# Expert layers: second-layer weights read by TensorE at a register's address in place of VectorE's copy

## The chip, the core and the metric

The kernel runs on one core of a Trainium2 chip. A core has five engines that run their own instruction streams and meet through semaphores: TensorE (PE; its weight loads are listed as PEld), VectorE (DVE), ScalarE (ACT), GpSimd (POOL) and SyncE (SP), which here issues transfers. Each engine has a sequencer in front of it that waits, branches, computes registers and issues; the profile writes a q behind the engine's name for it (DVEq, SPq, PEldq). The metric is the device time of one execution in microseconds (us).

## The reference, cut to what matters

The network has 14 blocks, four of them mixtures of experts: every token is sent to its best expert (first layer, `L0_ffn`, used twice) or to its best two (second layer, `L1_ffn`, used twice).

```
def _moe_mlp(x, gate_w, gate_b, w1, w2):                    # L0: 4096 tokens of 128, 8 experts, hidden 512
    one_hot = one_hot(argmax(xf @ gate_w + gate_b), E)
    h = gelu(einsum('td,edh->teh', xf, w1), approximate=True)
    y = einsum('teh,ehd->ted', h, w2)
    out = einsum('te,ted->td', one_hot, y)
...
def _moe(x, gate_w, gate_b, W1, b1, W2, b2):                # L1: the best two, weighted
    top_v, top_i = top_k(softmax(xt @ gate_w + gate_b), 2)
    for e in range(E):
        h = gelu(xt @ W1[e] + b1[e], approximate=False) @ W2[e] + b2[e]
        out = out + combine[:, e:e + 1] * h
```

The kernel holds x as 16 sequences of 256 tokens, 32 tiles of 128 tokens.

## The kernel before, in words

`experts` (L1237) is called four times: `e00_` and `e01_` with `top=1`, `e10_` and `e11_` with `top=2`. First it routes: each token's row goes by an indirect transfer to a place in the table `routed` in HBM, so that the rows of one expert lie together. Then comes the loop that this case is about, over NT tiles of 128 routed rows: NT is `TILES * top + 7`, 39 in e00 and e01, 71 in e10 and e11, 220 in all. The loops are written out in full. Which expert a tile belongs to is known only on the chip: `tables` writes it into `expert_i`, and the tile's place in `routed` into `offset_i`.

For tile j, named by what the trace writes:

- SP (L1353, L1354): waits until tile j-4 has been given out (`got` is a ring of four), loads the tile's place from `offset_i` into a register (a `value_load`: TENSOR_LOAD, FUSED_REGOPS, SEQ_ASSERT), and issues the transfer `e_got<-routed`.
- PE, one pass: `turn(j)` (L1734, e_F) waits for the transfer and transposes the rows; `hidden_layer(j-1)` (L1741, e_H) multiplies the tile before by `W1s`; `output(j-2)` (L1750, e_Y) multiplies the one before that by `W2s`. A float32 product of one block stands in the trace as two weight loads and two matmuls, so e_H and e_Y have eight each.
- ACT: copies e_F into `xT` (L1440, L1443) and applies the activation (L1449 in e00 and e01; L1453, four pieces with a bias, in e10 and e11).
- DVE, one pass: `weights(j)` loads the expert's number from `expert_i` into a register (L1601), copies the bias `b1s` (L1605, e10 and e11 alone), copies the expert's first layer from `core.W1` into `W1s` (L1608) and its second layer from `core.W2` into `W2s` (L1611), one of three buffers. Then `give(j-2)` makes the row addresses of the result (L1618, L1620, e_back), adds the second bias (L1624, e_biased, e10 and e11 alone) and writes `e_y` (L1628).
- POOL: sends `e_y` to the table `results` by an indirect transfer (L1397). After tiles 1, 5, 9 and so on to 29 it also adds a group of `core.Y` to `core.X` (L1401), and in e10 and e11 a bias row (L1406).

The stationary operand of e_Y is `hidden`; the weights of the second layer are the moving one. PE reads `W1s` and `W2s` at addresses that stand in the program. `core.W1` and `core.W2` hold all eight experts of a layer in SBUF.

Of the kernel before, what the change touches and what calls it, by code (L numbers as in the profile page):

```python
# [15 lines left out]
P = 128  # L16
SEQS, L, D = 16, 256, 128
# [44 lines left out]
def allocator(nc, ctx, prefix):  # L62

    held = []

    def clear():
        nc.clear_and_free_semaphores(held)
        nc.all_engine_barrier()

    ctx.callback(clear)  # L70

    def sb(name, shape, dt=F32):
        return ctx.enter_context(nc.sbuf_tensor(prefix + name, shape, dt))

    def ps(name, shape=(P, 512), dt=F32):
        return ctx.enter_context(nc.psum_tensor(prefix + name, list(shape), dt))

    def sig(name, per=1, lead=0):
        sem = nc.alloc_semaphore(prefix + name)
        held.append(sem)  # L80
        return Signal(sem, per, lead)

    return sb, ps, sig
# [49 lines left out]
def await_(eng, signal, count):  # L133
    if count > 0:
        eng.wait_ge(signal.sem, count)
# [1101 lines left out]
def experts(nc, core, name, *, affine, normed_in, w_loaded, gate, gate_b, act_fn, top, b1=None, b2=None,  # L1237
# [7 lines left out]
    E, FC = 8, 4  # L1245
# [4 lines left out]
    with ExitStack() as ctx:  # L1250
        sb, ps, sig = allocator(nc, ctx, name)
# [3 lines left out]
        YB = [ps("Y0"), ps("Y1")]  # L1255
# [28 lines left out]
        expert_i = sb("expert_i", [P, NT], I32)  # L1284
# [4 lines left out]
        got = sb("got", [P, RING, W])  # L1289
        xT = sb("xT", [P, 2, P])  # L1290
        W1s = sb("W1s", [P, 2, FC * P])
        W2s = sb("W2s", [P, 3, FC, D])
        b1s = sb("b1s", [P, 3, FC]) if b1 is not None else None
        b2_all = sb("b2_all", [P, E, D]) if b2 is not None else None
        biased = sb("biased", [P, 2, D]) if b2 is not None else None
# [1 line left out]
        hidden = sb("hidden", [P, 2, FC, P])  # L1297
# [15 lines left out]
        counted, count_made, offsets_made, tables_made = (sig("counted"), sig("count_made"), sig("offsets_made"),  # L1313
                                                          sig("tables_made"))
        fetched = [sig(f"fetched{b}") for b in range(RING)]
        x_made, x_taken = sig("x_made"), sig("x_taken")
        w1_copied, w2_copied, hid_made, acted, y_made, y_taken, back_ready = (
            sig("w1_copied"), sig("w2_copied"), sig("hid_made"), sig("acted"), sig("y_made"), sig("y_taken"),
            sig("back_ready"))
        given = sig("given")  # L1320
        y_sent = [sig(f"y_sent{b}") for b in range(RING)]
# [142 lines left out]
        def _(dve):  # L1464
            steps = 0

            def step(ins):
                nonlocal steps
                ins.then_inc(dve_step.sem, 1)
                steps += 1  # L1470

            def settle():
                dve.wait_ge(dve_step.sem, steps)
# [124 lines left out]
            expert = {}  # L1598

            def weights(j):  # L1600
                e = expert[j] = dve.value_load(expert_i[0:1, j:j + 1], min_val=0, max_val=E - 1)  # L1601
                await_(dve, hid_made, j - 1)
                if b1 is not None:
                    await_(dve, acted, j - 2)
                    step(dve.tensor_copy(b1s[:, j % 3], core.b1[:].rearrange("p (e f) -> p e f", e=E)  # L1605
                                         [:, bass.ds(e, 1), :].rearrange("p o f -> p (o f)")))
                    settle()
                dve.tensor_copy(W1s[:, j % 2], core.W1[:, bass.ds(e, 1), :].rearrange("p o f -> p (o f)"))\  # L1608
                    .then_inc(w1_copied.sem, 1)
                await_(dve, y_made, j - 2)  # L1610
                dve.tensor_copy(W2s[:, j % 3], core.W2[:, bass.ds(e, 1)].rearrange("p o c d -> p (o c) d"))\  # L1611
                    .then_inc(w2_copied.sem, 1)

            def give(j):

# [33 lines left out]
            for j in range(NT + 2):  # L1649
                if j < NT:  # L1650
                    weights(j)
                if j >= 2:
                    give(j - 2)
# [40 lines left out]
        @block.tensor  # L1694
        def _(pe):
            def rank_tokens(g):

                pe.wait_ge(chosen.sem, g + 1)
                pe.wait_ge(based.sem, g + 1)
                await_(pe, placed, g)  # L1700
                pe.matmul(RB[:, 0:GT * E], core.ones16[:], before16[:, g % 2, None, :].to_broadcast([P, GT, E]),
                          start=True, stop=False)
                for back_by in range(1, GT):
                    pe.matmul(RB[:, back_by * E:GT * E], core.ones16[:], taken_by[:, g % 2, 0:GT - back_by, :],
                              start=False, stop=False)
                pe.matmul(RB[:, 0:GT * E], core.earlier16[:], taken_by[:, g % 2], start=False, stop=True)\
                    .then_inc(ranked.sem, 1)

            for g in range(GROUPS + 1):
                if g >= 1:  # L1710
                    rank_tokens(g - 1)
                if g < GROUPS:
                    if normed_in:
                        pe.wait_ge(normed.sem, normed.at(g, GT))
                    await_(pe, h_taken, g - 1)
                    for t in range(GT):
                        src = rows[:, 0, g % 2, t, 0:D] if normed_in else core.Y[:, g * GT + t, :]
                        ins = pe.transpose(F[g % 2][:, t * P:(t + 1) * P], src, core.ident[:])
                    ins.then_inc(h_made.sem, 1)
                    pe.wait_ge(h_taken.sem, g + 1)  # L1720
                    await_(pe, logit_taken, g)
                    for t in range(GT):
                        ins = pe.matmul(LB[:, t * E:(t + 1) * E], hT[:, g % 2, t * P:(t + 1) * P], gate[:],
                                        start=True, stop=True)
                    ins.then_inc(logit_made.sem, 1)
            pe.wait_ge(placed.sem, GROUPS)
            pe.wait_ge(based.sem, GROUPS + 1)
            pe.matmul(RB[:, 0:E], core.ones16[:], before16[:, GROUPS % 2, :], start=True, stop=True)\
                .then_inc(count_made.sem, 1)

            def turn(j):
                pe.wait_ge(fetched[j % RING].sem, 16 * (j // RING + 1))
                await_(pe, x_taken, j - 1)
                pe.transpose(F[j % 2][:, 0:P], got[:, j % RING, 0:D], core.ident[:]).then_inc(x_made.sem, 1)  # L1734

            def hidden_layer(j):
                pe.wait_ge(x_taken.sem, j + 1)
                pe.wait_ge(w1_copied.sem, j + 1)
                await_(pe, acted, j - 1)
                for f in range(FC):  # L1740
                    ins = pe.matmul(H[j % 2][:, f * P:(f + 1) * P], W1s[:, j % 2, f * P:(f + 1) * P], xT[:, j % 2],  # L1741
                                    start=True, stop=True)
                ins.then_inc(hid_made.sem, 1)

            def output(j):
                pe.wait_ge(acted.sem, j + 1)
                await_(pe, y_taken, j - 1)
                pe.wait_ge(w2_copied.sem, j + 1)
                for f in range(FC):
                    ins = pe.matmul(YB[j % 2][:, 0:D], hidden[:, j % 2, f], W2s[:, j % 3, f, :],  # L1750
                                    start=f == 0, stop=f == FC - 1)
                ins.then_inc(y_made.sem, 1)

            for j in range(NT + 2):
                if j < NT:
                    turn(j)
                if 1 <= j <= NT:
                    hidden_layer(j - 1)
                if j >= 2:
                    output(j - 2)  # L1760
# [737 lines left out]
def network(nc, a, out):  # L2498
    core = Core()
    with ExitStack() as ctx:  # L2500
# [36 lines left out]
        def l0_experts(n, prefetch=None):  # L2537
            experts(nc, core, f"e0{n}_", affine=(col("L0_ffn_ln2_w"), col("L0_ffn_ln2_b")), normed_in=True,
                    w_loaded=(core.moe_loaded.sem, 32), gate=core.gates[:, 0, :], gate_b=core.gate_b[:, 0, :],
                    act_fn=ACT.Gelu_apprx_tanh, top=1, prefetch=prefetch)  # L2540

        def l1_experts(n):
            experts(nc, core, f"e1{n}_", affine=None, normed_in=False, w_loaded=(core.moe_loaded.sem, 64),
                    gate=core.gates[:, 1, :], gate_b=core.gate_b[:, 1, :], act_fn=ACT.Gelu, top=2,
                    b1=core.b1, b2=a["b2"], out_norm=(row("L1_ffn_ln2_g"), row("L1_ffn_ln2_b")))
# [147 lines left out]
```

## Time and profile before

| | us |
|---|---|
| median of 3 runs | 5303.79 |
| lowest and highest | 5299.88, 5307.32 |
| the profiled execution | 5306.9 |
| its span, first to last instruction | 5305.2 |

| engine | busy us | share of the span | instructions |
|---|---|---|---|
| PE | 3913.4 | 74% | 25840 |
| PEld | 2745.5 | 52% | 25840 |
| DVE | 3560.2 | 67% | 9744 |
| ACT | 2366.2 | 45% | 5537 |
| POOL | 2394.7 | 45% | 3900 |

No engine is busy all the time, and the 14 blocks follow one another with a barrier between them, so a change inside `experts` is read from the four stretches in which its loop runs. They lie at about 972 to 1078, 2192 to 2303, 3181 to 3407 and 5017 to 5247 us, some 674 us of the span. Busy time leaves out sequencer work (register operations, waits, issues); only the rows that are asked for by a source line show those.

### The profile page before, as it was taken

To read this page: it belongs to the slowest core of one execution; us is meant where nothing else is said; L and a number is where in the kernel's file an instruction comes from. 1 tells how busy PE (TensorE), PEld (TensorE's weight loads), DVE (VectorE), ACT (ScalarE), POOL (GpSimd) and SP (SyncE) were. 2 spreads that over 40 slices of the span, in tenths; PEclk is the share of its full clock that TensorE was granted. 3 is DMA by queue.
4 is the path that set the end of the run, shared out by engine and by line. 5 is a ranking of instruction groups with operands and counts; after the bars stand their busy time and mean duration, and the time that the engine had idled before them with its cause. 6 is when DMAs were issued, how large, how long until landed. Compare 5 with 4: busy or idle time off the path is not lost. (4 is left out here: it accounts for less than half of the span.)

```text
span 5305.2 us, 89506 instructions
## 1 busy us (share of the span) xinstructions
PE 3913.4 (74%) x25840; PEld 2745.5 (52%) x25840; DVE 3560.2 (67%) x9744; ACT 2366.2 (45%) x5537; POOL 2394.7 (45%) x3900
## 2 busy tenths in 40 slices
PE   5889786679999787558868826457786887787364
PEld 3666464556666465446646526422333664455263
DVE  5787675656666675656657757669997664676566
ACT  2444464255555465234435514345552553355142
POOL 3656442433343442446633244367775661232542
PEclk9999898889999899789979959879998999899597
DMA  5000232100000232133313211212222330232112
GB/s 218 0 0 0 95 115 80 43 24 1 1 0 1 81 115 77 38 114 108 104 70 108 90 38 40 64 48 62 64 64 69 111 106 1 87 107 72 41 40 74
DMA packets 243672, 341.35 MB, mean 64 GB/s; under 512 B 26848, under 2 KB 185968, under 8 KB 242224
## 3 DMA queue, kind: packets, MB, share of 16 engines
q1 hardware_dynamic: 230064, 309.19, 17.5%
q0 software_dynamic: 13184, 27.22, 1.5%
q8 instruction: 179, 2.93, 0.2%
q14 instruction: 245, 2.01, 0.1%
HBM read 182.77 MB, written 147.26 MB: 62 GB/s over the span
## 5 line engine op out<-in xcount | busy, mean ns | idle before, releaser
L507 DVE TENSOR_REDUCE l0att_rowmax<-l0att_S 128x2 f32<-128x512 f32 x512 | 339.7, 686 | 144.7 <-PE l0att_S L678 143.7
L507 DVE TENSOR_REDUCE l1ffn_rowmax<-l1ffn_S 128x2 f32<-128x512 f32 x512 | 340.9, 686 | 134.5 <-PE l1ffn_S L678 133.1
L869 POOL TENSOR_TENSOR wb_prob<-wb_prob,wb_rden 128x128 f32<-128x128 f32 (+1 forms) x512 | 248.9, 508 | 378.3 <-DVE wb_rden L1046 378.0
L1397 POOL DMA_INDIRECT results<-e_y,e_back x220 | 216.1, 982 | 417.0 <-DVE e_y L1628 398.2
L1943 POOL TENSOR_TENSOR ssm_hc<-core_AW_all,ssm_Cs 128x512 f32<-128x512 f32 x256 | 321.2, 1271 | 129.6 <-DVE core_AW_all L2089 96.5
L911 ACT ACTIVATE wb_prob<-wb_biased,wb_nmax 128x128 f32<-128x128 f32 (+1 forms) x512 | 228.6, 447 | 254.2 <-DVE wb_nmax L1039 251.3
L2188 PE MATMUL ssm_Y<-ssm_hc,core_ident 128*128 128x512 f32 x512 | 290.8, 679 | 56.0 <-POOL ssm_hc L1943 29.8
L678 PE MATMUL l1ffn_S<-l1ffn_K,l1ffn_Q 128*128 128x512 f32 x512 | 253.5, 499 | 96.2 <-DVE l1ffn_rowmax L507 58.7
L2089 DVE TENSOR_TENSOR_SCAN core_AW_all<-core_AW_all,ssm_U 128x512 f32<-128x512 f32 x256 | 310.2, 1212 | 1.4 <-ACT core_AW_all L2032 1.4
L678 PE MATMUL l0att_S<-l0att_K,l0att_Q 128*128 128x512 f32 x512 | 249.3, 490 | 59.7 <-DMA l0att_K<-bounce 52.1
L2032 ACT ACTIVATE core_AW_all<-ssm_dt,ssm_A 128x510 f32<-128x510 f32 x256 | 178.5, 716 | 221.6 <-DVE core_AW_all L2089 220.0
L1039 DVE CUSTOM_DVE_ANT_0 wb_biased<-wb_S,wb_added 128x128 f32<-128x128 f32 (+1 forms) x512 | 162.6, 355 | 168.1 <-PE wb_S L1142 124.2
L1382 POOL DMA_INDIRECT routed<-e_rows,e_pos_i x192 | 188.3, 981 | 155.2 <-DVE e_pos_i L1556 104.1
L1734 PE MATMUL e_F<-core_ident,e_got 128*128 128x128 f32 x220 | 73.2, 333 | 244.7 <-DMA e_got<-routed 232.5
L484 ACT ACTIVATE core_AW_all<-l1ffn_T 128x512 f32<-128x512 f32 x256 | 151.8, 597 | 211.0 <-PE l1ffn_T L691 209.1
L1741 PE MATMUL e_H<-e_xT,e_W1s 128*128 128x128 f32 x1760 | 245.9, 285 | 0.0
L1750 PE MATMUL e_Y<-e_W2s,e_hidden 128*128 128x128 f32 x1760 | 238.3, 280 | 0.7 <-ACT e_hidden L1453 0.7
L911 ACT ACTIVATE wa_prob<-wa_biased,wa_nmax 128x128 f32<-128x128 f32 (+1 forms) x256 | 114.3, 447 | 250.6 <-DVE wa_nmax L1039 250.5
L1741 PEld LDWEIGHTS e_H<-e_xT,e_W1s 128*128 128x128 f32 x1760 | 224.7, 200 | 0.4
L484 ACT ACTIVATE core_AW_all<-l0att_T 128x512 f32<-128x512 f32 x256 | 149.1, 597 | 163.9 <-PE l0att_T L691 162.1
L1750 PEld LDWEIGHTS e_Y<-e_W2s,e_hidden 128*128 128x128 f32 x1760 | 220.2, 197 | 1.2 <-ACT e_hidden L1453 1.1
L2082 DVE TENSOR_TENSOR ssm_U<-ssm_du,ssm_B 128x512 f32<-128x512 f32 x256 | 177.8, 695 | 57.3 <-POOL ssm_du L1934 38.0
(499 smaller groups left out, 11841.5 us busy)
## 6 DMA issues: line engine op xcount, KB each, us to landing
bounce<-l0att_parts SPq DMA_DIRECT2D x128, 256.0 KB, 2.8
bounce<-l1ffn_parts SPq DMA_DIRECT2D x128, 256.0 KB, 2.8
ssm_Cs<-c_rows SPq DMA_DIRECT2D x128, 256.0 KB
routed<-core_Y SPq DMA_DIRECT2D x8, 2048.0 KB, 23.5
l0att_Q<-bounce SPq DMA_DIRECT2D x128, 128.0 KB
l0att_K<-bounce SPq DMA_DIRECT2D x128, 128.0 KB
bounce<-l1att_parts SPq DMA_DIRECT2D x64, 256.0 KB, 2.8
l1ffn_Q<-bounce SPq DMA_DIRECT2D x128, 128.0 KB
```

The costliest lines, as they stand in the source:

```text
L484: act.activation(probT[jp][:, kt, m, :, q0:L], T[u % 4][:].rearrange("p (j q) -> p j q", j=2)[:, :, q0:L], ACT.Exp)\
L507: dve.tensor_reduce(out=rowmax[:, jp, qt, 2 * pair:2 * pair + 2], in_=S[a % 2][:].rearrange("p (j k) -> p j k", j=2)[:, :, 0:keys(qt)], op ...
L678: ins = pe.matmul(out[:, :, 0:keys(qt)], Q[:, n % 2, jp, pair, tile(qt)], K[:, n % 2, jp, :, pair, 0:keys(qt)], start=not causal, stop=Tru ...
L869: ins = pool.tensor_tensor(out=prob[:, w_ % 4, a:b], in0=prob[:, w_ % 4, a:b], in1=rden[:, w_ % 4, n:n + 1].to_broadcast([P, b - a]), op=A ...
L911: ins = act.activation(prob[:, w_ % 4, a:b], biased[:, w_ % 2, a:b], ACT.Exp, scale=-1.0, bias=nmax[:, w_ % 4, n:n + 1], accum_out=total[: ...
L1382: pool.indirect_dma_start(core.routed, bass.IndirectOffsetOnAxis(ap=pos_i[:, g % 2, k, t:t + 1], axis=0), rows[:, k, g % 2, t, :], None).t ...
L1397: pool.indirect_dma_start(core.results, bass.IndirectOffsetOnAxis(ap=back[:, j % RING, 1:2], axis=0), y[:, j % RING, :], None).then_inc(y_ ...
L1741: ins = pe.matmul(H[j % 2][:, f * P:(f + 1) * P], W1s[:, j % 2, f * P:(f + 1) * P], xT[:, j % 2], start=True, stop=True)
L1750: ins = pe.matmul(YB[j % 2][:, 0:D], hidden[:, j % 2, f], W2s[:, j % 3, f, :], start=f == 0, stop=f == FC - 1)
L1943: pool.tensor_tensor(out=hc[:, u % 4], in0=hs[:, u % 4], in1=Cs[:, n % 4], op=ALU.mult)\
L2089: dve.tensor_tensor_scan(hs[:, u % 4], dA[:, u % 4], BU[u % 2][:], 0.0, ALU.mult, ALU.add)\
L2188: pe.matmul(YS[c][:], core.ident[:], hc[:, u % 4], start=n == 0, stop=n == N - 1)\
```

## The change

The copy of the second layer's weights, its three buffers and its semaphore are taken out of VectorE's `weights(j)`. TensorE's matmuls of `output` take their moving operand from `core.W2` itself, at an address worked out from a register that holds the tile's expert. TensorE fills that register with a `value_load` of its own, for tile j right behind `turn(j)`, and waits once ahead of its loop for `offsets_made`.

```diff
-        W2s = sb("W2s", [P, 3, FC, D])
...
                 dve.tensor_copy(W1s[:, j % 2], core.W1[:, bass.ds(e, 1), :].rearrange("p o f -> p (o f)"))\
                     .then_inc(w1_copied.sem, 1)
-                await_(dve, y_made, j - 2)
-                dve.tensor_copy(W2s[:, j % 3], core.W2[:, bass.ds(e, 1)].rearrange("p o c d -> p (o c) d"))\
-                    .then_inc(w2_copied.sem, 1)
...
+            expert = {}
+
             def output(j):
+
+                e = expert.pop(j)
                 pe.wait_ge(acted.sem, j + 1)
                 await_(pe, y_taken, j - 1)
-                pe.wait_ge(w2_copied.sem, j + 1)
                 for f in range(FC):
-                    ins = pe.matmul(YB[j % 2][:, 0:D], hidden[:, j % 2, f], W2s[:, j % 3, f, :],
+                    ins = pe.matmul(YB[j % 2][:, 0:D], hidden[:, j % 2, f],
+                                    core.W2[:, bass.ds(e, 1), f, :].rearrange("p o d -> p (o d)"),
                                     start=f == 0, stop=f == FC - 1)
                 ins.then_inc(y_made.sem, 1)
 
+            pe.wait_ge(offsets_made.sem, 1)
             for j in range(NT + 2):
                 if j < NT:
                     turn(j)
+                    expert[j] = pe.value_load(expert_i[0:1, j:j + 1], min_val=0, max_val=E - 1)
                 if 1 <= j <= NT:
                     hidden_layer(j - 1)
                 if j >= 2:
```

On PE, in the steady part of the loop of e00, one pass stood like this before (F is the transpose, H the first layer, Y the second; ISA is a register operation):

```order
L1734 MATMUL e00_F0<-core_ident,e00_got 128x128
L1741 MATMUL e00_H1<-e00_xT,e00_W1s 128x128 x4
L1750 MATMUL e00_Y0<-e00_W2s,e00_hidden 128x128 x4
L1734 MATMUL e00_F1<-core_ident,e00_got 128x128
L1741 MATMUL e00_H0<-e00_xT,e00_W1s 128x128 x4
```

and stands like this with the change:

```order
L1730 MATMUL e00_F0<-core_ident,e00_got 128x128
L1758 TENSOR_LOAD e00_expert_i
L1758 ISA x2
L1737 MATMUL e00_H1<-e00_xT,e00_W1s 128x128 x4
L1749 ISA
L1749 MATMUL e00_Y0<-core_W2,e00_hidden 128x128
L1749 ISA
L1749 MATMUL e00_Y0<-core_W2,e00_hidden 128x128
L1749 ISA
L1749 MATMUL e00_Y0<-core_W2,e00_hidden 128x128
L1749 ISA
L1749 MATMUL e00_Y0<-core_W2,e00_hidden 128x128
```

Three instructions now stand between the transpose and the first layer, and one register operation ahead of each matmul of the second layer.

On DVE, one pass of e10 stood like this before:

```order
L1601 TENSOR_LOAD e10_expert_i
L1601 ISA x2
L1605 ISA
L1605 COPY e10_b1s<-core_b1 128x4
L1608 ISA
L1608 COPY e10_W1s<-core_W1 128x512
L1611 REGISTER_ALU
L1611 COPY e10_W2s<-core_W2 128x512
L1618 TENSOR_TENSOR e10_back<-e10_got,e10_keep_i 128x1
```

and with the change:

```order
L1600 TENSOR_LOAD e10_expert_i
L1600 ISA x2
L1604 ISA
L1604 COPY e10_b1s<-core_b1 128x4
L1607 ISA
L1607 COPY e10_W1s<-core_W1 128x512
L1614 TENSOR_TENSOR e10_back<-e10_got,e10_keep_i 128x1
```

The copy and its register operation are gone; VectorE still loads the expert's number itself. ACT, POOL and SP keep their instructions.

## Rows read from the trace of the kernel before

**Rows 1.** The loop of e00: who waited for whom, total us, times, longest.

```profile
PE e_F L1734 <- DMA e_got<-routed: 29.1, 23, 9.3
DVE e_y L1628 <- PE e_Y L1750: 22.1, 20, 1.8
```

**Rows 2.** In time order, e00: start us, us, engine line op, [idle before <-releaser].

```profile
1016.44 1.06 PE L1750 MATMUL e_Y<-e_W2s,e_hidden 128*128 128x128 f32 x8
1017.53 0.35 DVE L1628 TENSOR_SCALAR e_y<-e_Y,e_got 128x128 f32<-128x128 f32 x1 [0.42 <-PE e_Y L1750]
1018.28 0.43 DVE L1608 COPY e_W1s<-core_W 128x512 f32 x1 [0.40 <-issue]
1018.80 0.33 PE L1734 MATMUL e_F<-core_ident,e_got 128*128 128x128 f32 x1 [1.30 <-DVE e_W1s L1608]
1018.96 1.07 PE L1741 MATMUL e_H<-e_xT,e_W1s 128*128 128x128 f32 x8
1019.86 1.06 PE L1750 MATMUL e_Y<-e_W2s,e_hidden 128*128 128x128 f32 x8
1020.76 0.27 PE L1734 MATMUL e_F<-core_ident,e_got 128*128 128x128 f32 x1
...
1024.02 0.33 PE L1734 MATMUL e_F<-core_ident,e_got 128*128 128x128 f32 x1 [1.20 <-DMA e_got<-routed]
```

**Rows 3.** SP's value_load by its line, one tile: ns min/median/max, start us.

```profile
L1353 SPq TENSOR_LOAD <-e_offset_i x1: 268/268/268, 1005.3 to 1005.3; - x1
L1353 SPq FUSED_REGOPS  x1: 152/152/152, 1005.6 to 1005.6; - x1
L1353 SPq SEQ_ASSERT  x1: 18/18/18, 1005.8 to 1005.8; - x1
L1354 SPq FUSED_REGOPS  x1: 42/42/42, 1005.9 to 1005.9; - x1
```

**Rows 4.** VectorE's value_load by its line, one tile, and the e_y ahead of it.

```profile
1006.73 0.35 DVE L1628 TENSOR_SCALAR e_y<-e_Y,e_got 128x128 f32<-128x128 f32 x1 [0.16 <-issue]
L1601 DVEq TENSOR_LOAD <-e_expert_i x1: 302/302/302, 1006.7 to 1006.7; - x1
L1601 DVEq FUSED_REGOPS  x1: 190/190/190, 1007.1 to 1007.1; - x1
L1608 DVEq FUSED_REGOPS  x1: 57/57/57, 1007.4 to 1007.4; - x1
```

**Rows 5.** PE's sequencer by line: waits of e00's loop, register operations of another block.

```profile
L135 PEldq EVENT_SEMAPHORE  x1: 51/51/51, 1018.8 to 1018.8; - x1
L1748 PEldq EVENT_SEMAPHORE  x1: 51/51/51, 1018.9 to 1018.9; - x1
L821 PEldq FUSED_REGOPS  x12: 50/50/50, 119.7 to 1591.4; - x12
L821 DVEq FUSED_REGOPS  x12: 62/63/69, 120.3 to 1595.8; - x12
```

**Rows 6.** DVE in time order, loop of e10, two passes of a group of four.

```profile
3255.85 0.61 DVE L1608 COPY e_W1s<-core_W 128x512 f32 x1
3256.39 0.41 DVE L1611 COPY e_W2s<-core_W 128x512 f32 x1
3256.71 0.15 DVE L1618 TENSOR_TENSOR e_back<-e_got,e_keep_i 128x1 uint32<-128x1 uint32 x1
...
3261.16 0.17 DVE L1605 COPY e_b1s<-core_b 128x4 f32 x1 [0.55 <-issue]
3261.47 1.98 DVE L1608 COPY e_W1s<-core_W 128x512 f32 x1
3263.38 1.50 DVE L1611 COPY e_W2s<-core_W 128x512 f32 x1
3264.80 0.14 DVE L1618 TENSOR_TENSOR e_back<-e_got,e_keep_i 128x1 uint32<-128x1 uint32 x1
```

**Rows 7.** PE in time order: the ends of that group, and two tiles further on.

```profile
3254.99 0.33 PE L1734 MATMUL e_F<-core_ident,e_got 128*128 128x128 f32 x1 [2.76 <-DMA e_got<-routed]
...
3268.51 0.33 PE L1734 MATMUL e_F<-core_ident,e_got 128*128 128x128 f32 x1 [2.93 <-DMA e_got<-routed]
...
3295.65 0.33 PE L1734 MATMUL e_F<-core_ident,e_got 128*128 128x128 f32 x1 [2.89 <-DMA e_got<-routed]
...
3301.28 0.33 PE L1734 MATMUL e_F<-core_ident,e_got 128*128 128x128 f32 x1 [0.59 <-DMA e_got<-routed]
```

**Rows 8.** POOL in time order, in the same group.

```profile
3261.88 1.28 POOL L1401 TENSOR_TENSOR core_X<-core_X,core_Y 128x512 f32<-128x512 f32 x1
3263.24 1.35 POOL L1406 TENSOR_TENSOR core_X<-core_X,core_rows 128x512 f32<-128x512 f32 x1
```

More of the change, by code:

```diff
@@ L1316, in experts @@
         x_made, x_taken = sig("x_made"), sig("x_taken")
-        w1_copied, w2_copied, hid_made, acted, y_made, y_taken, back_ready = (
-            sig("w1_copied"), sig("w2_copied"), sig("hid_made"), sig("acted"), sig("y_made"), sig("y_taken"),
+        w1_copied, hid_made, acted, y_made, y_taken, back_ready = (
+            sig("w1_copied"), sig("hid_made"), sig("acted"), sig("y_made"), sig("y_taken"),
             sig("back_ready"))
```

## The prediction

> **What bounds the kernel now.** The change touches only the expert loops, so I read the list of waits inside one loop first, then the time order of each engine there. The waits of e00 [rows 1] show that PE is not short of work but of data: before 23 of its 39 transposes (e_F) it sits idle until the fetched rows land, 29.1 us in all, while DVE waits for PE's e_Y in 20 passes. Neither is the bound by itself. They form a ring with SP's transfer, because `got` has four buffers and the fetch of tile j+4 waits until tile j has been given out. Follow it in [rows 2]. PE's pass with e_F at 1018.80 ends its e_Y at 1020.92 (1019.86 + 1.06), so the PE part is 2.12 us. From the end of an e_Y to the e_F that it lets go: e_Y of 1016.44 ends at 1017.50, e_y is written from 1017.53 to 1017.88, and the transpose of that chain starts at 1020.76 at the latest, with the one at 1024.02 following from the e_Y that ended at 1020.92. That is 3.10 to 3.26 us. The ring spans two tiles (tile j is given out in the pass of tile j+2 and releases tile j+4), so a tile costs (2.12 + 3.15) / 2 = 2.64 us, near what the passes at 1018.80, 1020.76 and 1024.02 show: 5.22 us for two. PE alone could do a pass in 1.96 us.
>
> In e10 and e11 DVE has more to do. In the first 32 tiles the groups of four take 13.52 us (3254.99 to 3268.51) [rows 7]. In one pass of each group DVE's two copies stretch from 0.61 and 0.41 us to 1.98 and 1.50 us [rows 6], and both end 0.3 us after one of POOL's additions does [rows 8]. Behind them everything on DVE is late, e_y with it, and PE waits 2.93 us. Past tile 32 POOL adds nothing, and the ring rules: 3295.65 to 3301.28 is 5.63 us for two tiles, 2.82 each.
>
> **The change, part by part.**
>
> *Taken from DVE.* One copy a tile. Without a stall it holds up the next instruction for 0.32 us (3256.39 to 3256.71 [rows 6]), with one for 1.42 us (3263.38 to 3264.80). In e00 and e01 that buys nothing: DVE idles 0.42 us ahead of the e_y of 1017.53, waiting for PE [rows 2], and it is PE that it waits for in 20 passes [rows 1]. Past tile 32 in e10 and e11 the ring rules as well. In the 16 groups of the first 32 tiles (8 in each of e10, e11) DVE is the late one: its chain of 13.52 us loses 3 x 0.32 + 1.42 = 2.4 us and comes to 11.1 us a group. What is late next there is the ring, below. The first-layer copy keeps its stall of about 1.4 us.
>
> *The lock.* Both stretched copies end 0.3 us behind a POOL addition [rows 6, 8]. The Trainium skill ("SBUF — State Buffer", section "Who interferes with whom") says that a VectorE copy in a 2-port mode and a GpSimd instruction exclude each other for a whole instruction; by that rule, and the trace agrees, one of the two stalls in each group goes with the copy and the other stays.
>
> *Put on PE: the value_load.* Three sequencer instructions a tile, behind e_F and ahead of e_H. No row shows them on PE, so I bound them by the two engines that do them. On SP they take 268, 152 and 18 ns, 0.44 us bare; with the gaps between them, from the start of the load at 1005.3 to the next instruction at 1005.9, some 0.57 us [rows 3]. On DVE it is 0.64 us (1006.7 to 1007.4) [rows 4]. I take SP's 0.57, since for one and the same register operation PE needs 50 ns where DVE needs 63 [rows 5], so PE's sequencer is of the quicker kind. The ends are 0.44 and 0.64.
>
> *Is it hidden?* A pass hides it only if the sequencer can do it while PE still works or still waits. DVE's load starts at 1006.7, when the wait of the e_y ahead of it is over (1006.73) and not before [rows 4]. On PE the wait instruction that stands behind e_F runs at 1018.8, with the e_F of 1018.80 itself [rows 5, 2], though what it waits for besides had nearly all come earlier. So I take it that the sequencer stands at e_F until the rows have landed, and the load begins then. PE has emptied its queue by that time (it was idle 1.30 us), so e_H starts 0.57 us later than now. Even a pass such as that of 1020.76, with no idle time ahead, began about when its rows landed, since each fetch goes out right behind an e_y. I count the load in full in nearly every pass.
>
> *Put on PE: four register operations* ahead of the matmuls of e_Y, some 50 ns each [rows 5] with a gap like SP's 40 ns, 0.09 us apiece and 0.36 us in all. The sequencer now comes by ahead of e_Y (L1748) at 1018.9, while its first matmul starts at 1019.86 [rows 5, 2]: a lead of 0.9 us, because e_H runs for 0.9 us in between. The load moves both alike, so the lead stays and covers them. If the cover were gone they would cost 0.36 us a pass. The moving operand's size stays, so the eight matmuls keep their pace: nothing. The wait for `offsets_made` stands ahead of transposes that wait for transfers which wait for it as well: nothing.
>
> *The sum.* 0.57 us more in PE's part of a ring over two tiles is 0.285 us a tile.
> - e00 and e01: 78 tiles x 0.285 = +22 us.
> - e10 and e11 past tile 32: 78 x 0.285 = +22 us.
> - e10 and e11, first 32 tiles: the ring is now 2.82 + 0.285 = 3.10 us a tile, 12.4 us a group, and covers DVE's 11.1. Against 13.52 that is -1.1 x 16 groups = -18 us.
> - Sum +26 us. A few passes whose rows land early hide the load; I take 1 off: +25. On the profiled execution's 5306.9 that is 5332; the median is 3.1 lower, so 5329.
>
> With 0.44 us the terms are +17, +17 and -1.4 x 16 = -22: +12. With 0.64: +25, +25 and -1.0 x 16 = -16: +34. So 5316 to 5338 for this case.
>
> **The rivals.**
>
> *The load runs while e_F waits (faster).* If the sequencer only hands e_F to a queue and goes on, the load is over when the rows land, at least where PE was idle. For it: PE's sequencer does come by ahead of e_Y 0.9 us early. Against it: the two starts above. Then the e00, e01 and late terms are 0, and a group falls to the ring's 4 x 2.82 = 11.3 us or DVE's 11.1, less gain where the remaining stall shows: -1.7 to -2.2 x 16 = -28 to -36, so about 5273. The Trainium skill ("Perfetto Trace Analysis", section "Tensor Engine Instruction") describes just this: the sequencer pushes an instruction into a wait queue and is ready for the next before the semaphore is met. DVE's load in [rows 4] doesn't start as early as that would let it. 13%.
>
> *The address operations are not covered (slower still).* A matmul whose operand is at a register's address may be taken one at a time, each behind its register operation. Then 0.36 us a pass comes on top, 0.18 us a tile, x 220 = +40: 5370. It decides when one matmul with its operation takes the sequencer longer than the 0.22 us that PE needs for a block, and the lead of 0.9 us is used up. No row shows such a matmul. 14%.
>
> *The load costs less, or DVE's relief reaches further.* The loss in 156 tiles and the gain in 64 pull against each other; with 0.35 us of load exposed the terms are +14, +14 and -1.6 x 16 = -25, about +3: 5307. 13%.
>
> **How the numbers follow.** The forecast, 5316 to 5338, gets 60%; the three rivals 13, 14 and 13%. Predicted 5329, the likeliest case's time. The range of 5296 to 5372 takes in all but the hidden load (13%) and some 5% above. A change of 0.2%, 10.6 us, is about what a measurement of this kernel can tell from none. Slower by more: the forecast and the second rival, nearly whole, 73%. Within: the third, 13%. Faster: the first and a little of the third, 14%.
>
> **What would show it.** In the changed kernel PEldq would have TENSOR_LOAD, FUSED_REGOPS and SEQ_ASSERT of about 268, 152 and 18 ns, the first starting with e_F; from e_F to the first e_H 0.73 us, where it is 0.16 now [rows 2]; e_H to e_Y still 0.90 us; two tiles in the ring of e00 about 5.8 us in place of 5.2; the loops of e00 and e01 some 11 us longer each. The groups of four in e10 would take about 12.4 us, with one stretched copy each. Wrong would be a load that starts before e_F, an e_H to e_Y distance of over 1 us, or a lower granted clock in the loops, where PE would now idle more; that the sum leaves out.

## The result and the profile after

The changed kernel takes 5340.99 us (median of 5) against 5304.12 (5299.88 to 5312.59) of the kernel before beside it: a ratio of 1.0064, 95% interval 1.0048 to 1.0080. Slower by 0.6%, where 5329 had been predicted. (One execution of the five, of 5540.77 us with a granted clock of 0.781 on average, stands outside the comparison.) The profiled execution took 5331.7 us, its span 5330.0, so +24.8 on the span of before. The sum of the prediction was +25, but that match is partly luck. The profiled execution is the fastest of the changed kernel (the others within the comparison took 5339.8 to 5345.4); the medians lie 37 us apart, and 5341 is 3 us above the prediction's 5316 to 5338 for its likeliest case, inside its range of 5296 to 5372. And the two parts of the profiled difference are both off.

I measure a loop from the start of its first e_F to the end of its last e_y. In e10 and e11, "front" is from the e_F of tile 2 to that of tile 34, "tail" from there to tile 70.

| us | before | after | difference | predicted |
|---|---|---|---|---|
| e00 | 106.7 | 121.6 | +14.9 | +11 |
| e01 | 111.2 | 119.0 | +7.8 | +11 |
| e10, of it front, tail | 226.5, 111.2, 106.1 | 242.8, 110.5, 121.9 | +16.3, -0.7, +15.8 | front -9, tail +11 |
| e11, of it front, tail | 230.3, 114.6, 106.3 | 242.0, 111.6, 119.9 | +11.7, -3.0, +13.6 | front -9, tail +11 |
| four loops | 674.7 | 725.4 | +50.7 | +26 |
| everything else | 4630.5 | 4604.6 | -25.9 | 0 |

Two things had not been foreseen: the loops lost twice as much as the sum says, and 26 us came back in parts of the program that the change doesn't touch.

What the load and the address operations do to PE stands in the rows of their lines in the kernel after (operation, count, ns min/median/max, first and last start; L1758 is the value_load, L1749 the e_Y matmuls):

```profile
L1758 PEldq TENSOR_LOAD <-e_expert_i x220: 295/300/497, 975.8 to 5266.4; - x110
L1758 PEldq FUSED_REGOPS  x220: 146/151/165, 976.4 to 5266.7; - x110
L1758 PEldq SEQ_ASSERT  x220: 18/18/28, 976.6 to 5266.9; - x110
...
L1749 PE MATMUL e_Y<-core_W,e_hidden x1760: 274/275/423, 981.3 to 5272.2; 128*128 x196
L1749 PEldq FUSED_REGOPS  x880: 46/46/56, 980.3 to 5271.6; - x176
```

And in time order, two passes of e00, PE alone (start us, us, engine line op, idle time before):

```profile
1016.18 0.33 PE L1730 MATMUL e_F<-core_ident,e_got 128*128 128x128 f32 x1 [1.57 <-DMA e_got<-routed]
1016.92 1.13 PE L1737 MATMUL e_H<-e_xT,e_W1s 128*128 128x128 f32 x8 [0.41 <-issue]
1017.89 1.06 PE L1749 MATMUL e_Y<-core_W,e_hidden 128*128 x8
1018.78 0.27 PE L1730 MATMUL e_F<-core_ident,e_got 128*128 128x128 f32 x1
1018.89 1.06 PE L1737 MATMUL e_H<-e_xT,e_W1s 128*128 128x128 f32 x8
...
1022.02 0.33 PE L1730 MATMUL e_F<-core_ident,e_got 128*128 128x128 f32 x1 [1.17 <-DMA e_got<-routed]
```

The loads of these two passes, by the value_load's line in two short windows:

```profile
L1758 PEldq TENSOR_LOAD <-e_expert_i x1: 299/299/299, 1016.2 to 1016.2; - x1
...
L1758 PEldq TENSOR_LOAD <-e_expert_i x1: 297/297/297, 1017.8 to 1017.8; - x1
```

The first e_F had waited 1.57 us for its rows. Its load starts with it, at 1016.2, and e_H comes 0.74 us later instead of 0.16 [rows 2]. The rows of the second pass had landed already. Its load starts at 1017.8, a full microsecond ahead of its e_F, and e_H follows e_F in 0.11 us. So the sequencer is held by the wait for the rows, not by the transpose. All 220 loads bear this out: none starts before the last signal of its tile's transfer, and half of them start within 0.04 us of it. In most pairs of passes of e00, one pass shows the load and the other hides it: 2.60 us from e_F to e_F and then 3.24, where before it was 1.96 and 3.26 [rows 2]. Averaged over the passes, e_F to e_H went from some 0.16 us to 0.49, 0.52, 0.58 and 0.57 in the four loops; it is 0.6 us or more in 44 of the 76 passes of e00 and e01, and in 83 of the 140 of e10 and e11.

The stall that was to vanish with the W2s copy didn't. POOL and DVE in e10, kernel after, in time order:

```profile
3265.93 1.99 DVE L1607 COPY e_W1s<-core_W 128x512 f32 x1
3266.35 1.28 POOL L1400 TENSOR_TENSOR core_X<-core_X,core_Y 128x512 f32<-128x512 f32 x1
...
3267.70 1.34 POOL L1405 TENSOR_TENSOR core_X<-core_X,core_rows 128x512 f32<-128x512 f32 x1
3267.84 1.22 DVE L1614 TENSOR_TENSOR e_back<-e_got,e_keep_i 128x1 uint32<-128x1 uint32 x1
```

The little e_back operation, 0.14 us otherwise, stands where W2s stood in [rows 6], and takes 1.22 us beside POOL's second addition. Its row for the whole run has a longest of 1849 ns in the kernel after and of 158 in the kernel before; in the fronts of e10 and e11 it is stretched 8 times each, as often as the W2s copy was.

```profile
L1614 DVE TENSOR_TENSOR e_back<-e_got,e_keep_i x220: 140/142/1849, 980.1 to 5271.6; 128x1 uint32<-128x1 uint32 x110
```

```profile
L1618 DVE TENSOR_TENSOR e_back<-e_got,e_keep_i x220: 140/147/158, 976.3 to 5246.5; 128x1 uint32<-128x1 uint32 x110
```

The Trainium skill ("SBUF — State Buffer", section "Who interferes with whom") states this case too: a VectorE instruction with two SBUF inputs contends with a GpSimd instruction that reads SBUF. The trace agrees (1.22 us against 0.14), and the prediction had used only the part of that section on copies.

The granted clock in the loops fell as well. PE's busy time, the clock (PEclk) and the DMA share in the four loops, first before and then after:

```profile
972.00:1079.00 107.00, 82.68 (x663) 0.98 0.17 48
2192.00:2303.00 111.00, 82.62 (x663) 0.97 0.17 46
3181.00:3408.00 227.00, 154.47 (x1207) 0.98 0.15 42
5017.00:5248.00 231.00, 159.10 (x1207) 0.95 0.15 41
```

```profile
975.00:1097.00 122.00, 90.59 (x663) 0.94 0.15 42
2193.00:2312.00 119.00, 90.02 (x663) 0.95 0.15 43
3186.00:3429.00 243.00, 172.33 (x1207) 0.93 0.14 39
5031.00:5273.00 242.00, 170.99 (x1207) 0.94 0.14 39
```

Counted by the distance between neighbouring matmuls of e_H and e_Y (0.112 us at 2.4 GHz, some 0.22 at 1.2), 191 steps ran at the lower level before and 501 after. In the experiments below, the kernels with the load behind the transpose have 499 to 543 such steps (354 where filler matmuls are added); those without it, or with it ahead, have 116 to 344.

The 26 us outside the loops: 18.0 of them lie in the wide attention block between e00 and e01 (tensors wb_), a block with a real loop that the engines jump back in. From its first to its last matmul it takes 654.6 us before and 636.6 after. Its DVE rows at one such jump, before and after (ALU_OP and COMPARE_BRANCH end a turn, FUSED_REGOPS begins the next):

```profile
L821 DVEq ALU_OP  x1: 45/45/45, 1347.5 to 1347.5; - x1
L821 DVEq COMPARE_BRANCH  x1: 63/63/63, 1347.6 to 1347.6; - x1
L821 DVEq FUSED_REGOPS  x1: 63/63/63, 1350.6 to 1350.6; - x1
...
1350.92 0.29 DVE L1039 CUSTOM_DVE_ANT_0 wb_biased<-wb_S,wb_added 128x128 f32<-128x128 f32 x1 [2.72 <-PE wb_S L1142]
```

```profile
L821 DVEq ALU_OP  x1: 40/40/40, 1361.7 to 1361.7; - x1
L821 DVEq COMPARE_BRANCH  x1: 56/56/56, 1361.8 to 1361.8; - x1
L821 DVEq FUSED_REGOPS  x1: 63/63/63, 1362.1 to 1362.1; - x1
...
1362.61 0.29 DVE L1039 CUSTOM_DVE_ANT_0 wb_biased<-wb_S,wb_added 128x128 f32<-128x128 f32 x1 [0.22 <-PE wb_S L1142]
```

The jump back takes 0.3 us after and 3.0 before. All five jumps of each run are alike: 2.78 to 2.97 us before, 0.30 to 0.33 after. Summed over the five, the jumps are 12.8 us shorter. The remaining 5 us go along with a granted clock of 0.98 in that loop before and 1.00 after (window, DVE busy, PEclk, DMA share, GB/s; before, then after). 
```profile
1264.00:1690.00 426.00, 273.84 (x1161) 0.98 0.00 1
```

```profile
1264.00:1690.00 426.00, 285.47 (x1212) 1.00 0.00 0
```

Nothing in this block was changed. What differs is that DVE has 78 instructions fewer ahead of it in the trace (39 copies of W2s and 39 operations for their address). The jumps of PE, ACT and POOL at the same place take the same time in both kernels (0.27, 0.23 and 0.16 us).

### The profile page after: what moved, and what is told of

Same layout as the page of the kernel before. It is cut to its first block and busy times, and to the rows that moved or that the text cites. A ratio compares the mean times of both kernels' runs of the same rounds, so it can differ in the third digit from the quotient of the medians.

```text
span 5330.0 us, 90602 instructions
## 1 busy us (share of the span) xinstructions
PE 3936.0 (74%) x25840; PEld 2761.6 (52%) x25840; DVE 3490.3 (65%) x9524; ACT 2362.8 (44%) x5537; POOL 2390.6 (45%) x3900
## 5 line engine op out<-in xcount | busy, mean ns | idle before, releaser
L678 PE MATMUL l1ffn_S<-l1ffn_K,l1ffn_Q 128*128 128x512 f32 x512 | 251.4, 495 | 95.7 <-DVE l1ffn_rowmax L507 52.0
L1737 PE MATMUL e_H<-e_xT,e_W1s 128*128 128x128 f32 x1760 | 267.3, 299 | 59.1 <-ACT e_xT L1442 32.0
L1039 DVE CUSTOM_DVE_ANT_0 wb_biased<-wb_S,wb_added 128x128 f32<-128x128 f32 (+1 forms) x512 | 162.8, 356 | 150.6 <-PE wb_S L1142 106.7
L1749 PE MATMUL e_Y<-core_W,e_hidden 128*128 x1760 | 247.4, 287 | 0.9 <-ACT e_hidden L1452 0.9
L1452 ACT ACTIVATE e_hidden<-e_H,e_b1s 128x128 f32<-128x128 f32 x568 | 162.4, 368 | 165.9 <-PE e_H L1737 165.9
L1749 PEld LDWEIGHTS e_Y<-core_W,e_hidden 128*128 128x128 f32 x1760 | 229.6, 204 | 1.5 <-issue 1.4
```

What stands on the lines that cost most here:

```text
L678: ins = pe.matmul(out[:, :, 0:keys(qt)], Q[:, n % 2, jp, pair, tile(qt)], K[:, n % 2, jp, :, pair, 0:keys(qt)], start=not causal, stop=Tru ...
L1749: ins = pe.matmul(YB[j % 2][:, 0:D], hidden[:, j % 2, f], core.W2[:, bass.ds(e, 1), f, :].rearrange("p o d -> p (o d)"), start=f == 0, sto ...
```

## The experiments

Theory at the start: the load, exposed behind a transpose that waits, makes the loops slower; hidden, the kernel would be no slower than before. Rivals: the address operations; the granted clock; the stalls; and, for the block outside, chance, the freed buffer or the place of the code.

**The load alone, and where it stands.** Four kernels. load_only adds an unused load to the kernel before:

```diff
+            pe.wait_ge(offsets_made.sem, 1)
             for j in range(NT + 2):
                 if j < NT:
                     turn(j)
+                    pe.value_load(expert_i[0:1, j:j + 1], min_val=0, max_val=E - 1)
```

> The kernel before, with PE's value_load of each tile's expert added behind the transpose and its result unused; VectorE's copy and its buffers stay. It isolates the load. Theory of the prediction (the load begins when the fetched rows land and delays e_H by 0.57 to 0.64 us, half of which a ring over two tiles passes on, 0.29 to 0.32 us a tile): e00 and e01 +22 to +25 us together, e10 and e11 past tile 32 +22 to +25, their first 32 tiles nearly nothing since VectorE is late there anyway: +44 to +50 us, near 5350. Rival (the loss comes from the register operations and matmuls at register addresses in e_Y): within 10 us of the kernel before. If the granted clock falls in the loops as in the changed kernel (0.93 to 0.95 where it was 0.95 to 1.00), some 15 us come on top.

Measured: 5393.90 us (5383.8 to 5400.1), ratio 1.0155 (1.0131 to 1.0180); loops 745.8 us, +71.1. This rules out that the loss comes from the matmuls at register addresses alone, since this kernel has none. The load by itself costs more than the whole change, and more than expected: I had left the fronts of e10 and e11 out, as bound by DVE, and they rose from 111.2 and 114.6 to 122.3 and 122.2. Against it, the changed kernel's 725.4 says what the copy's removal gives once the load is exposed: 20 us, 11 in each front.

idle_load_ahead has the same unused load ahead of `turn(j)`:

```diff
+            pe.wait_ge(offsets_made.sem, 1)
             for j in range(NT + 2):
                 if j < NT:
+                    pe.value_load(expert_i[0:1, j:j + 1], min_val=0, max_val=E - 1)
                     turn(j)
```

> The kernel before with the same unused value_load, but ahead of the transpose instead of behind it, so that the sequencer does it while the matmuls of the pass before run. Theory of the prediction: it is over before the rows land, so nothing is exposed: 5304, within 5 us. Rival (a register load on PE costs wherever it stands, by emptying the queue): +40 us, as load_only.

Measured: 5323.42 us (5309.3 to 5335.9), ratio 1.0023 (1.0010 to 1.0036); loops 686.7. Hidden, but some 12 us slower where 5 at most were expected. In the one profile the loops are 12 us longer, about what the two tails rose by (113.1 and 111.1 us against 106.1 and 106.3). But two profiles of the next kernel, load_ahead, have loops of 679.5 and 665.7 us, 14 apart, so that one profile can't place these 12 us. What costs them stays open.

load_ahead is the changed kernel with the two lines exchanged:

```diff
                 if j < NT:
-                    turn(j)
                     expert[j] = pe.value_load(expert_i[0:1, j:j + 1], min_val=0, max_val=E - 1)
+                    turn(j)
```

> The changed kernel with its value_load moved from behind turn(j) to ahead of it; nothing else. It keeps the four register operations and the matmuls at register addresses. Theory of the prediction: the load is hidden, what is left is VectorE's relief in the first 32 tiles of e10 and e11, 1.0 to 1.7 us a group of four, 16 groups: 16 to 28 us under the kernel before, 5276 to 5288. Rival (the address operations and dynamic matmuls cost by themselves, 0.18 us a tile): 5310 or more.

Measured: 5284.09 us (5274.0 to 5303.3), ratio 0.9958 (0.9943 to 0.9973). e_F to e_H is 0.16 us on average again, though all 220 loads and 880 address operations are there. The time is as expected, but not for the reason given: it was to come from 16 to 28 us less in the loops, and they took 679.5 us in this profile, 5 more than before. The gain lies in the block outside, below. Run once more (below) it gave 0.9956. PE in e00 of that second run, and its loads:

```profile
1016.04 0.33 PE L1730 MATMUL e_F<-core_ident,e_got 128*128 128x128 f32 x1 [1.33 <-DMA e_got<-routed]
1016.21 1.06 PE L1737 MATMUL e_H<-e_xT,e_W1s 128*128 128x128 f32 x8
1017.11 1.06 PE L1749 MATMUL e_Y<-core_W,e_hidden 128*128 x8
1018.00 0.27 PE L1730 MATMUL e_F<-core_ident,e_got 128*128 128x128 f32 x1
...
L1757 PEldq TENSOR_LOAD <-e_expert_i x2: 297/345/393, 1016.8 to 1018.6; - x2
```

The loads start at 1016.8 and 1018.6, while PE works off e_H and e_Y. This rules the address operations out as a cost of any size: they are the same here.

double_load is the changed kernel with a second load behind the first.

```diff
                     expert[j] = pe.value_load(expert_i[0:1, j:j + 1], min_val=0, max_val=E - 1)
+                    pe.value_load(expert_i[0:1, j:j + 1], min_val=0, max_val=E - 1)
```

> The changed kernel with its value_load behind the transpose done twice. Theory of the prediction (what stands behind the landing of the rows is exposed in full, and half of it is passed on): e_F to e_H grows from 0.71 to about 1.3 us and the time by 0.29 to 0.32 us a tile, 220 tiles: +65 to +70 us over the changed kernel, some 5405. Rival (much of the load lies beside other work): +20 us or less.

Measured: 5415.05 us (5404.2 to 5421.0), ratio 1.0199 (1.0176 to 1.0222); loops 790.9 us, +65.4 on the changed kernel. e_F to e_H is now 1.15, 1.16, 1.07 and 0.98 us. The second load is no longer hidden in the second pass of a pair:

```profile
1016.61 1.06 PE L1749 MATMUL e_Y<-core_W,e_hidden 128*128 x8
1017.50 0.27 PE L1730 MATMUL e_F<-core_ident,e_got 128*128 128x128 f32 x1
1018.62 1.13 PE L1737 MATMUL e_H<-e_xT,e_W1s 128*128 128x128 f32 x8 [0.85 <-ACT e_xT L1439]
```

The theory held (+65 to +70 us expected). A second load costs the loops 0.30 us a tile (65.4 / 220), half of its 0.57 us, as a ring over two tiles should have it, and with as many steps at the lower clock (499) as the changed kernel has.

**The granted clock.** after_fill gives PE two idle matmuls a pass.

```diff
                 if j >= 2:
                     output(j - 2)
+                if 2 <= j < NT:
+                    for _ in range(2):
+                        pe.matmul(LB[:, 0:P], core.ident[:], core.ident[:], start=True, stop=True)
```

> The changed kernel with two idle matmuls (128x128 by the identity into the free bank e_L) behind the second layer of every pass from the third on. PE works where it would wait. Theory (the load's stop at each transpose costs part of its time through the granted clock: 501 of the loops' matmul steps run at half speed after the change, 191 before): the count of half-speed steps falls below 250, the granted clock of the loops rises from .93 to .95 to .98 or more, and the loops, which take 725 us in all, come down by 15 to 30 us; time 5310 to 5328. Rival (the half-speed stretches lie where PE waits anyhow, or the fillers' own 0.2 us a pass take the gain back): loops 720 to 745 us, time 5336 to 5361.

Measured: 5346.27 us (5338.3 to 5351.9), ratio 1.0078 (1.0056 to 1.0099). The four loops, where the clock of the last rose from 0.94 to 0.98:

```profile
974.00:1098.00 124.00, 103.21 (x802) 0.95 0.15 41
2191.00:2317.00 126.00, 104.31 (x803) 0.95 0.15 40
3200.00:3445.00 245.00, 194.54 (x1474) 0.95 0.14 39
5050.00:5294.00 244.00, 190.56 (x1477) 0.98 0.14 39
```

Slow steps fell from 501 to 354, short of the 250 expected, and the loops took 738.1 us, 13 more, about as much as two profiles of one kernel can differ by. The rival came true: the loops didn't get shorter (that the fillers took what the clock gave is likely, not shown). How much of the loss is the clock's this run can't say.

**The stalls.** Three kernels move POOL's additions onto core_X behind the tile loop: the kernel before, the changed kernel, and the one with the load ahead.

```diff
-                if j % 4 == 1 and j // 4 < GROUPS:
-                    g = j // 4
-                    pool.tensor_tensor(out=group(core.X, g), in0=group(core.X, g), in1=group(core.Y, g), op=ALU.add)\
+            for g in range(GROUPS):
+                pool.tensor_tensor(out=group(core.X, g), in0=group(core.X, g), in1=group(core.Y, g), op=ALU.add)\
...
```

> The kernel before with POOL's additions behind the tile loop. Theory (before the change the two stalls of each group, W1s 1.98 and W2s 1.50 us, made VectorE the late one in the first 32 tiles of e10 and e11): no stretched copy is left, and those 32 tiles fall from 111.2 and 114.6 us to the pace of the last 36, 2.95 us a tile, so 93 to 97 us each. Rival (the stalls sit in slack): 107 to 114 us.

> The changed kernel with POOL's additions onto core_X behind the tile loop instead of one group in every fourth pass. Theory (after the change the stall that W2s had taken is handed to e_back, the next VectorE instruction with two SBUF inputs, 1.22 us instead of 0.14, and W1s keeps its own, 1.99): without the additions no W1s copy and no e_back in e10 and e11 is stretched, and the first 32 tiles of e10 and e11 (110.5 and 111.6 us now) run like the rest, 3.05 to 3.3 us a tile: 98 to 106 us each. The additions then cost about 16 x 2.6 = 42 us behind each loop, so the whole is slower, 5370 to 5410. Rival (the groups of four are bound by the ring with the load in it, not by the stalls): the first 32 tiles stay at 108 to 112 us.

> The kernel with the load ahead of the transpose and POOL's additions behind the tile loop. Theory (with the load hidden, the stalls of W1s, 1.99 us, and of e_back, 1.22 us, which has taken W2s's place, are what keep the first 32 tiles at 108 to 114 us): without the additions 91 to 97 us, as in the kernel before without them, so that the going copy brought nothing but another victim for the stall. Rival (the ring or the rows that the earlier load delays): 104 to 112 us.

Measured, one execution each: 5319.35, 5381.46 and 5284.45 us. The additions now stand bare behind each loop, so the time to look at is that of the fronts. No W1s copy and no e_back is stretched in any of them; these are the changed kernel's rows with the additions moved, to be held against the 1849 ns above and a longest W1s of 2245:

```profile
L1606 DVE COPY e_W1s<-core_W x220: 426/598/617, 973.1 to 5303.5; 128x512 f32 x110
L1613 DVE TENSOR_TENSOR e_back<-e_got,e_keep_i x220: 139/141/159, 977.1 to 5307.9; 128x1 uint32<-128x1 uint32 x110
```

| front of e10, e11, us | additions in the loop | behind it | tail of e10, e11 |
|---|---|---|---|
| before | 111.2, 114.6 | 97.4, 96.1 | 105.0, 105.4 |
| changed kernel | 110.5, 111.6 | 109.4, 109.4 | 120.4, 118.3 |
| load ahead (first run) | 110.5, 113.6 | 94.9, 95.7 | 106.9, 105.6 |

The front of e10 in the last of them, tile 2 to tile 34:

```profile
3174.99 0.42 PE L1729 MATMUL e_F<-core_ident,e_got 128*128 128x128 f32 x1
...
3269.84 0.33 PE L1729 MATMUL e_F<-core_ident,e_got 128*128 128x128 f32 x1 [1.67 <-DMA e_got<-routed]
```

For before and for the load ahead my theory held: the stalls cost some 16 us a front, with the W2s copy and without it, so the copy's going only gave the stall another victim. Moving the additions also takes them out of the way of POOL's own transfers, which these runs don't part from the stalls; but in the front of e10 before, no row has DVE waiting for POOL. For the changed kernel the rival held: with the load exposed the ring sets the pace, 3.42 us a tile, stalls or none.

**The block outside the loops.** ahead_pad is the kernel with the load ahead, and on DVE behind e00's loop:

```diff
+            if name == "e00_":
+                for _ in range(78):
+                    dve.wait_ge(offsets_made.sem, 1)
```

ahead_held is the same kernel with a tensor and a signal held in the place of W2s and w2_copied, unused.

> The kernel with the load ahead of the transpose, plus 78 waits on a signal long given, on VectorE behind the tile loop of e00: as many instructions as the removed copies and their register operations were in e00. Theory (the 18 us that the wide attention block behind e00 gains in every kernel without the copy come from where its VectorE loop lies in the instruction stream): that block takes 652 to 657 us, as in the kernels with the copy, instead of 636.6, and the whole 5298 to 5308. Rival (they come from the room or the signal that the copy had held, or from something else): 635 to 639 us, whole 5284 to 5291.

> The kernel with the load ahead of the transpose, plus a tensor of the size of the removed buffers at their place and a signal at the place of w2_copied, neither used. Theory of the instruction stream: nothing moves, the wide attention block behind e00 takes 635 to 639 us and the whole 5278 to 5290. Rival (addresses or numbers of signals made the difference of 18 us): 652 to 657 us, whole 5296 to 5308.

Measured: 5293.60 and 5274.25 us, one execution each; the block takes 656.9 and 636.8 us. In the trace the 78 waits are 39 instructions, two waits in each, so half of what was removed; it was enough. A jump back, first of ahead_pad, then of ahead_held:

```profile
L821 DVEq COMPARE_BRANCH  x1: 63/63/63, 1352.0 to 1352.0; - x1
L821 DVEq FUSED_REGOPS  x1: 63/63/63, 1354.8 to 1354.8; - x1
```

```profile
L821 DVEq COMPARE_BRANCH  x1: 56/56/56, 1350.1 to 1350.1; - x1
L821 DVEq FUSED_REGOPS  x1: 63/63/63, 1350.4 to 1350.4; - x1
```

The same kernel with 39 idle instructions ahead of the block has the long jump and the 20 us back. Buffer and signal do nothing. That the place of DVE's code decides is shown; why, is not. Over the fourteen profiles, all four kernels in which DVE keeps the copy of W2s and its code as it was, and the two padded ones, take 654 to 657 us, and the others without the copy 636 to 637.

I then tried to give the same to the kernel before. before_pad adds 178 waits (four a tile and 22 behind the loop of e00).

> The kernel before, plus 178 waits on a signal long given on VectorE in e00 (four ahead of each wait for y_made, where VectorE waits for PE anyhow, and 22 behind the loop). Nothing else is changed; VectorE still copies both layers. Theory (only the place of the wide attention block's VectorE loop in the instruction stream decides its jump back, 0.3 us or 2.8 us; 178 more is the place of the changed kernel, 78 fewer, if places 256 apart are alike): the block takes 635 to 639 us in place of 654.6, each jump about 0.3 us, and the whole comes to 5284 to 5292 with no change to the experts. Rival (places 256 apart are not alike, or the copy's going itself did it): the block stays at 652 to 657 us and the whole at 5303 to 5312.

> The kernel with the load ahead of the transpose once more, beside the kernel before with shifted code. It was 5284.1 us (5274.0 to 5303.3), 0.9958 of before. Theory (its whole gain of some 20 us is the block's 18 us and next to nothing is left from VectorE's relief): within 0.15% of the time of before_pad. Rival (the relief of VectorE is worth something by itself, as the loops of 662 to 680 us against 675 let hope): 8 to 20 us under before_pad.

Measured: before_pad 5308.08 us (5295.7 to 5328.4), ratio 0.9997 (0.9983 to 1.0011), the block 655.5 us. The waits came to 89 instructions, not 178, so the place I wanted was not reached, and the question whether the kernel before could have the 18 us with no change to the experts stays open. Beside it load_ahead_again took 5288.84 us (5276.1 to 5295.8), ratio 0.9956 (0.9941 to 0.9971): -23 us, of which the block is 18. Against before_pad it is 19 us, as its rival had it (8 to 20); but before_pad has the long jumps still, and the theory had been worked out for short ones, so that the comparison doesn't decide between them. The loops of load_ahead_again took 665.7 us, against 674.7 and 670.3 in the two kernels with the copy; the four runs of the load-ahead kernel and its padded and held forms have 679.5, 665.7, 666.6 and 661.6. What the copy's going is worth to the loops is thus some 5 us, no more than they scatter.

## Why the prediction was right, and where it was right by accident

- **The load's price.** 300, 151 and 18 ns on PE against 268, 152 and 18 assumed; e_F to e_H 0.74 us against 0.73 where it is exposed. Right.
- **Exposed in nearly every pass.** Wrong: in 127 of 216 passes e_F to e_H is 0.6 us or more. In e00 the second pass of a pair mostly hides it, since the sequencer is free as soon as the rows have landed. The Trainium skill ("Perfetto Trace Analysis", section "Tensor Engine Instruction") has the sequencer push an instruction into a wait queue and go on. The trace agrees where the rows were there (load at 1017.8, e_F at 1018.78) and not where they weren't (1016.2 and 1016.18). One exposed load for two tiles gives the same 0.285 us a tile as the prediction's account, so e00 and e01 came out at +22.7 us where +22 stood. They did so as +14.9 and +7.8, at a lower granted clock, which the sum leaves out; so close a match is partly luck.
- **The address operations covered.** Right: e_H to e_Y is 0.97 us in the exposed pass and 0.90 in the other, and the kernel with the load ahead shows no cost of them. On average e_H to e_Y is 0.99, 1.00, 1.05 and 1.05 us in the four loops, against 0.92 to 0.97 before, so the prediction's sign of being wrong (over 1 us) came up in e10 and e11. It isn't the address operations: load_only has none, and 1.00 to 1.07 us.
- **The tails**, +29.4 us for +22. The term rests on a ring of 2.82 us a tile, read at one pair [rows 7]; over the tail it is 2.95. In the trace the ring is from e_F of tile j+2 to the end of e_y of tile j, and from there to e_F of tile j+4. The first part grew from 3.04 to 3.58 us in e10 and 2.98 to 3.56 in e11, 0.41 of it the load, some 0.15 slower matmuls; the second from 2.87 to 3.19 and 2.92 to 3.06. Half the sum is 3.39 and 3.31 us, as the tails show (121.9 / 36 and 119.9 / 36). The prediction had the second part unchanged. What lengthened it I haven't separated.
- **The fronts**, -3.7 us for -18. This is the step that failed. It said that DVE's chain loses 2.4 us a group, 1.42 of it a stall, and that the ring is next at 12.4. The stall went over to e_back, and the ring with the load stands at 13.7 us a group (109.4 / 8, no stalls); a group takes 13.8 us in e10 (110.5 / 8). The ring was taken too short to begin with: without stalls the kernel before takes 12.2 and 12.0 us a group (97.4 / 8, 96.1 / 8), where the prediction had 4 x 2.82 = 11.3.
- **The granted clock.** Left out of the sum, named as what would make it wrong. It fell (191 to 501 slow steps). An estimate from these rows: 310 more steps, each 0.11 us longer, are 34 us of PE's time, of which a ring over two tiles would pass on half, 17 us. No run shows its part of the loss, which stays open.
- **Everything else at nothing.** Wrong by 25.9 us, 18 of them shown to hang on the place of DVE's code; the rest, 8 us ahead of e11, is within what other runs of these kernels differ by there (1602 to 1615 us for that stretch).

So the loops lost 51 us and not 26, and code that the change only moved gave back what had been missed. Had the block not gained, the time would have been about 5359, still inside the range.

The first rival (a load that hides itself, 5273) describes the load of the kernel with that line one higher, at 5284 and 5289, but not its gain: 28 to 36 us were to come from the fronts, which took 1.7 and 8.3 us less in its two profiles, and the 18 us of the block are most of what it won.

## What to carry to other kernels

A register load on an engine that waits for data belongs ahead of that wait, where the engine still has work queued: one line's place was worth 1% here (5341 against 5284 to 5289). A stall of VectorE beside a POOL operation is not removed with the instruction that shows it; look at what the next VectorE instruction in that place will do beside the same POOL operation. And when a change to unrolled code alters a part that it doesn't touch, look at the jumps of the real loops behind it before crediting the change.

## What the runs showed of the hardware that was not expected

- A DVE jump back over a turn of 364 traced instructions takes 0.30 us or 2.8, by where the code lies: 39 idle instructions ahead of it make the difference (636.6 or 656.9 us for the block). With it COMPARE_BRANCH itself is listed with 56 or 63 ns in the four jumps behind the first, which tells the two apart at a glance.
- PE's sequencer waits for a transpose's rows before it takes up a register load, but not for the transpose: the load starts with e_F when the rows are late, and ahead of it when they aren't (by 1.02 us in the pass shown). None of the 220 loads starts before its tile's rows have landed.
- A DVE operation of 128x1, with two SBUF inputs, takes up to 1.85 us beside a POOL addition, against 0.14.
- The register addresses of e_Y's 880 blocks cost 46 ns each on PE's sequencer and nothing on the path that could be seen, with e_Y's pace unchanged at 0.112 us a step.
